# The 16-head transformer of a four-stage kernel: order of the down product, the scores, the residual sum and the keys' sum within a pair of slots

## The reference

```python
def local_attention(q, k, v):          # windows of w = 32, keys of this and the last window
    ...
    sim = jnp.einsum('bhwie,bhwje->bhwij', bq, bk2) * QK_SCALE
    sim = jnp.where(mask, -jnp.finfo(sim.dtype).max, sim)
    attn = jax.nn.softmax(sim, -1)
    out = jnp.einsum('bhwij,bhwje->bhwie', attn, bv2)
    ...
def attn_layer(x, Wqkv, qs, ksc, Wo):
    ...
    q = l2norm(q) * qs
    k = l2norm(k) * ksc
    ...
    q = q * cos * scale + rotate_half(q) * sin * scale
    k = k * cos * inv + rotate_half(k) * sin * inv
    out = local_attention(q, k, v)
    ...
    return out @ Wo
def ffn_layer(x, g, bln, W1, b1, W2, b2):
    mu = x.mean(-1, keepdims=True)
    var = ((x - mu) ** 2).mean(-1, keepdims=True)
    xn = (x - mu) / jnp.sqrt(var + 1e-05) * g + bln
    hg = xn @ W1 + b1
    a, gate = jnp.split(hg, 2, -1)
    return a * jax.nn.gelu(gate, approximate=False) @ W2 + b2
for i in range(DEPTH):
    x = attn_layer(shift_tokens(x), Wqkv[i], q_scale[i], k_scale[i], Wo[i]) + x
    x = ffn_layer(shift_tokens(x), ln_g[i], ln_b[i], W1[i], b1[i], W2[i], b2[i]) + x
```

## Time and profile before

| what | value |
|---|---|
| median of 3 runs | 3959.9 us (3956.89 to 3961.77) |
| the profiled execution | 3960.3 us, its span 3958.6 us |
| mean granted clock of TensorE | 0.963 |
| PE, DVE, ACT, POOL busy over the span | 89%, 63%, 58%, 45% |
| the touched stage | 1489.3 to 3319.3 us of the span (first and last maximum of the scores) |
| a pair of slots in it | about 19.0 us |

### The profile page before, as it was taken

How to read it: one execution, slowest core, us unless ns; L and a number is a source line. 1 busy time by engine, 2 the same in 40 slices (tenths; PEclk the granted TensorE clock), 3 DMA queues, 4 the chain that set the end, 5 groups by cost and what they waited for, 6 DMA issues and landing times. The chain is left out here.

```text
span 3958.6 us, 124976 instructions
## 1 busy us (share of the span) xinstructions
PE 3533.2 (89%) x52653; PEld 2411.9 (61%) x52653; DVE 2475.5 (63%) x5535; ACT 2290.3 (58%) x4664; POOL 1779.9 (45%) x1846
## 2 busy tenths in 40 slices
PE   7986999998999978999999999999999996968886
PEld 4664555544666645666666666666666665846664
DVE  4436554511666646776777777777677774568885
ACT  2233555522455546676666676666667665447775
POOL 2003000001011226666666666666666663167773
PEclk9997999998899989999999999999999998989998
DMA  0000000010000012112112112211211111121010
GB/s 26 2 3 24 1 1 1 1 30 7 2 2 2 2 35 74 46 45 71 45 47 69 46 47 56 61 47 45 71 46 46 45 46 27 30 78 24 21 23 20
DMA packets 156330, 130.09 MB, mean 33 GB/s; under 512 B 53592, under 2 KB 146304, under 8 KB 154880
## 3 DMA queue, kind: packets, MB, share of 16 engines
q1 hardware_dynamic: 155776, 122.09, 12.0%
HBM read 31.93 MB, written 3.54 MB: 9 GB/s over the span
## 5 line engine op out<-in xcount | busy, mean ns | idle before, releaser
L1072 PE MATMUL t_wa<-t_w_qkv,t_resid 128*128 128x512 f32 x1152 | 596.0, 617 | 22.3 <-DMA t_scales<-in_L_ffn_k_scale 18.9
L1387 DVE TENSOR_REDUCE t_nmax<-t_S 128x8 f32<-128x512 f32 x192 | 132.8, 692 | 358.6 <-PE t_S L1094 358.0
L1221 ACT ACTIVATE t_sq<-t_wa 128x512 f32<-128x512 f32 x384 | 216.3, 589 | 162.3 <-PE t_wa L1072 162.3
L1027 POOL TENSOR_TENSOR t_ra<-t_ra,t_rb 128x512 f32<-128x512 f32 x192 | 243.8, 1270 | 119.8 <-DVE t_rb L1345 119.8
L1327 DVE TENSOR_REDUCE t_ssq<-t_sq 128x8 f32<-128x512 f32 x384 | 261.0, 680 | 46.1 <-ACT t_sq L1221 46.1
L3079 DVE TENSOR_REDUCE a_nmax<-a_A 128x2 f32<-128x1024 f32 (+3 forms) x256 | 206.1, 822 | 127.0 <-PE a_A L2977 124.7
L1140 PE MATMUL t_misc<-t_oT,t_w_o 128*128 128x128 f32 x1536 | 194.2, 280 | 97.2 <-DVE t_resid L1376 97.2
L1256 ACT ACTIVATE t_oT<-t_T 128x512 f32<-128x512 f32 x192 | 114.8, 598 | 280.4 <-PE t_T L1129 280.3
L1020 POOL TENSOR_TENSOR t_rstd<-t_vare,half 128x1 f32<-128x1 f32 x96 | 52.9, 551 | 481.1 <-DVE t_vare L1398 481.1
L1110 PEld LDWEIGHTS t_T<-ident,t_ra 128*128 128x128 f32 x1536 | 177.3, 141 | 139.4 <-issue 105.0
L1072 PEld LDWEIGHTS t_wa<-t_w_qkv,t_resid 128*128 128x128 f32 x1152 | 188.1, 196 | 119.4 <-issue 95.3
(11 more groups left out here) (506 smaller groups left out, 9841.5 us busy)
## 6 DMA issues: line engine op xcount, KB each, us to landing
t_vw<-t_vn SPq DMA_DIRECT2D x768, 66.0 KB
t_vw<-t_vn SPq DMA_DIRECT2D x672, 33.0 KB
t_w_qkv<-in_L_ffn_Wqkv SPq DMA_DIRECT2D x6, 1536.0 KB, 6.6
t_v<-t_vn SPq DMA_DIRECT2D x56, 132.0 KB, 2.3
t_vw<-t_nothing SPq DMA_DIRECT2D x96, 33.0 KB
t_w_o<-in_L_ffn_Wo SPq DMA_DIRECT2D x6, 512.0 KB
f_h<-t_L_ffn_h_w SPq DMA_DIRECT2D x2, 1024.0 KB, 7.3
t_w<-in_L_ffn_W SPq DMA_DIRECT2D x6, 341.0 KB
```

The costliest lines, as they stand in the source:

```text
L1027: pool.tensor_tensor(ra[:, ahead % 2, 0], ra[:, ahead % 2, 0], rb[:, ahead % 2, 0], ALU.add).then_inc(q_added.sem, 1)
L1072: pe.matmul(bank, resid[:, b, lo:lo + P], w_qkv[:, l % 2, at:at + 512], start=True, stop=True).then_inc(wa_up.sem, 1)
L1221: act.activation(sq[:, r].rearrange("p h d -> p (h d)"), wa[:, WA[kind], :], ACT.Square).then_inc(squared.sem, 1)
```

## The change

No operation is added or taken away; the order of steps changes on three engines.

PE: in an even slot down comes ahead of turn_p instead of behind it. gate_up is cut into half_up(gate) and half_up(up), and the scores of the next (even) slot stand between the two, at the end of the odd slot, instead of at the head of the even one.

ACT, even slots: copy_q moves between the two squares, and copy_k ahead of the roots.

DVE, even slots: add_ffn moves from behind floor to behind the queries' sum, ahead of rotate_queries; the keys' sum and floor move behind the outputs; normalise_keys moves into the following odd slot, behind add_heads. In odd slots make_tables moves from the head of the slot to behind normalise_keys.

```diff
--- before.py
+++ after.py
@@ -1149,14 +1149,13 @@
                     pe.wait_ge(lnd.sem, lnd.at(t, 4))
                     pe.transpose(lnP, ln[:, :], ident[:, :]).then_inc(lnT_up.sem, 1)
 
-                def gate_up(t):
-                    l = layer_of(t)
+                def half_up(t, kind):
+                    l, half = layer_of(t), int(kind == "gate")
                     pe.wait_ge(lnT_in.sem, lnT_in.at(t, 1))
-                    for half, kind in ((1, "gate"), (0, "up")):
-                        bank = turn_bank(kind, t)
-                        for c in range(NH):
-                            m = pe.matmul(bank[:, c * P:(c + 1) * P], w_1[:, l % 2, half, c * P:(c + 1) * P], lnT[:, :], start=True, stop=True)
-                        m.then_inc(T_up.sem, 1)
+                    bank = turn_bank(kind, t)
+                    for c in range(NH):
+                        m = pe.matmul(bank[:, c * P:(c + 1) * P], w_1[:, l % 2, half, c * P:(c + 1) * P], lnT[:, :], start=True, stop=True)
+                    m.then_inc(T_up.sem, 1)
 
                 def down(t):
                     l = layer_of(t)
@@ -1166,7 +1165,7 @@
                     m.then_inc(f_up.sem, 1)
 
                 for even, now, turn, mid, ahead, tail, ffn, last in slots():
-                    if now is not None:
+                    if now is not None and (not even or last is None):
                         score(now)
                     if ahead is not None:
                         project("q", ahead)
@@ -1177,10 +1176,10 @@
                     if turn is not None:
                         turn_qk("q", turn)
                     if even:
+                        if last is not None:
+                            down(last)
                         if now is not None:
                             turn_p(now)
-                        if last is not None:
-                            down(last)
                         if turn is not None:
                             turn_qk("k", turn)
                         if now is not None:
@@ -1205,7 +1204,10 @@
                         if now is not None:
                             turn_o(now)
                         if ffn is not None:
-                            gate_up(ffn)
+                            half_up(ffn, "gate")
+                            if now is not None and now + 1 < TG:
+                                score(now + 1)
+                            half_up(ffn, "up")
 
             @block.scalar
             def _(act):
@@ -1274,13 +1276,18 @@
                             exponentials(now)
                         if ahead is not None:
                             square("q", ahead)
-                            square("k", ahead)
                         if turn is not None:
                             copy_q(turn)
+                        if ahead is not None:
+                            square("k", ahead)
                         if now is not None:
                             copy_p(now)
                         if mid is not None:
                             copy_v(mid)
+                        if turn is not None:
+                            copy_k(turn)
+                        if ahead is not None:
+                            roots(ahead)
                     else:
                         if ahead is not None:
                             square("q", ahead)
@@ -1294,10 +1301,10 @@
                             copy_q(turn)
                         if mid is not None:
                             copy_v(mid)
-                    if ahead is not None:
-                        roots(ahead)
-                    if turn is not None:
-                        copy_k(turn)
+                        if ahead is not None:
+                            roots(ahead)
+                        if turn is not None:
+                            copy_k(turn)
                     if ffn is not None:
                         norm_turned(ffn)
                     if now is not None:
@@ -1376,45 +1383,68 @@
                         v.scalar_tensor_tensor(out=resid[rows, b, cols], in0=fT[rows], scalar=b_2[rows, l % 2, :],
                                                in1=resid1[rows, b, cols], op0=ALU.add, op1=ALU.add).then_inc(tile_done.sem, 1)
 
+                def weights(G):
+                    scores = S[:, :, 0:4 * KEYS].rearrange("p r (h k) -> p r h k", h=4)
+                    v.wait_ge(scored.sem, scored.at(G))
+                    v.tensor_reduce(nmax[:, :, :], scores, X, ALU.max).then_inc(maxed.sem, 1)
+                    v.wait_ge(maxed.sem, maxed.at(G))
+                    v.tensor_tensor(p.rearrange("p j r k -> p r j k"), scores, spread(nmax[:, :, :], 3, KEYS), ALU.subtract).then_inc(subbed.sem, 1)
+
+                def outputs(G):
+                    out = S[:, :, 0:4 * VD].rearrange("p r (h d) -> p r h d", h=4)
+                    v.wait_ge(weighed.sem, weighed.at(G))
+                    v.reciprocal(rden[:, :, :], out[:, :, :, HD]).then_inc(recip.sem, 1)
+                    v.wait_ge(recip.sem, recip.at(G))
+                    v.tensor_tensor(o.rearrange("p j r d -> p r j d"), out[:, :, :, 0:HD], spread(rden[:, :, :], 3, HD), ALU.mult).then_inc(o_in.sem, 1)
+
+                def statistics(t):
+                    v.wait_ge(sh2_up.sem, sh2_up.at(t))
+                    v.bn_stats(stats[:, :], sh2).then_inc(lnd.sem, 1)
+                    v.wait_ge(lnd.sem, lnd.at(t, 1))
+                    v.bn_aggr(mv[:, :], stats[:, :]).then_inc(lnd.sem, 1)
+                    v.wait_ge(lnd.sem, lnd.at(t, 2))
+                    v.tensor_scalar(vare[:, :], mv[:, 1:2], LN_EPS, None, ALU.add).then_inc(lnd.sem, 1)
+
                 for even, now, turn, mid, ahead, tail, ffn, last in slots():
-                    if ahead is not None and ahead % SLOTS == 0:
-                        make_tables(layer_of(tile_of(ahead)))
-                    if ffn is not None:
-                        add_heads(ffn)
-                    if now is not None:
-                        scores = S[:, :, 0:4 * KEYS].rearrange("p r (h k) -> p r h k", h=4)
-                        v.wait_ge(scored.sem, scored.at(now))
-                        v.tensor_reduce(nmax[:, :, :], scores, X, ALU.max).then_inc(maxed.sem, 1)
-                        v.wait_ge(maxed.sem, maxed.at(now))
-                        v.tensor_tensor(p.rearrange("p j r k -> p r j k"), scores, spread(nmax[:, :, :], 3, KEYS), ALU.subtract).then_inc(subbed.sem, 1)
-                    if last is not None:
-                        gated(last)
-                    if ffn is not None:
-                        v.wait_ge(sh2_up.sem, sh2_up.at(ffn))
-                        v.bn_stats(stats[:, :], sh2).then_inc(lnd.sem, 1)
-                        v.wait_ge(lnd.sem, lnd.at(ffn, 1))
-                        v.bn_aggr(mv[:, :], stats[:, :]).then_inc(lnd.sem, 1)
-                        v.wait_ge(lnd.sem, lnd.at(ffn, 2))
-                        v.tensor_scalar(vare[:, :], mv[:, 1:2], LN_EPS, None, ALU.add).then_inc(lnd.sem, 1)
-                    if ahead is not None:
-                        sums("q", ahead)
-                    if ahead is not None:
-                        rotate_queries(ahead)
-                        sums("k", ahead)
-                        floor(ahead)
-                    if last is not None:
-                        add_ffn(last)
-                    if ffn is not None:
-                        v.wait_ge(rooted.sem, rooted.at(ffn))
-                        v.tensor_scalar(ln[:, :], sh2, mv[:, 0:1], rstd[:, 0:1], ALU.subtract, ALU.mult).then_inc(lnd.sem, 1)
-                    if now is not None:
-                        out = S[:, :, 0:4 * VD].rearrange("p r (h d) -> p r h d", h=4)
-                        v.wait_ge(weighed.sem, weighed.at(now))
-                        v.reciprocal(rden[:, :, :], out[:, :, :, HD]).then_inc(recip.sem, 1)
-                        v.wait_ge(recip.sem, recip.at(now))
-                        v.tensor_tensor(o.rearrange("p j r d -> p r j d"), out[:, :, :, 0:HD], spread(rden[:, :, :], 3, HD), ALU.mult).then_inc(o_in.sem, 1)
-                    if ahead is not None:
-                        normalise_keys(ahead)
+                    if even:
+                        if now is not None:
+                            weights(now)
+                        if last is not None:
+                            gated(last)
+                        if ahead is not None:
+                            sums("q", ahead)
+                        if last is not None:
+                            add_ffn(last)
+                        if ahead is not None:
+                            rotate_queries(ahead)
+                        if now is not None:
+                            outputs(now)
+                        if ahead is not None:
+                            sums("k", ahead)
+                            floor(ahead)
+                    else:
+                        if ffn is not None:
```

(21 more changed lines are left out.)

## The result

The changed kernel takes 3853.3 us, the median of four runs at 3846.5, 3847.9, 3858.6 and 4089.6 us, of which the last ran at a granted clock of 0.83 and is left out of the comparison. The kernel before took 3958.4 in the runs beside it. The ratio of the changed kernel's time to that of the one before is 0.973, its 95% interval 0.9705 to 0.9755: 107 us less, where 95 were forecast. The profiled execution took 3847.9 us.

What follows compares the result with a forecast made beforehand. PE was taken to bound the stage, idle mainly ahead of L1140 for DVE's late residual. 94 pairs by 1.07 us, less 6 for the tables, gave 94.6 off 3960.3: 3865 us, bounds 3855 to 3878, range 3850 to 3895.

Steps and rivals of the forecast that it cites:

- the replay: One pair's steps retimed on its own clock from profile durations: pair goes from 19.05 to 17.98 us.
- The sum's main term: PE's wait ahead of head product L1140 goes: 1.07 us in each of 94 pairs, 100.6 us.
- The 0.21: Weigh's start behind copy_p's end in the kernel before, read as ACT's copy fixing that start.
- The tables: make_tables behind normalise_keys on DVE costs about 1.2 us in each of five pairs, 6 us.
- the lower bound of my sum: 96 pairs winning 1.10 us each and no cost of the tables: 3855 us.
- the margin that I left below: The range was the forecast's 3855 to 3878, extended down to 3850.
- weigh is bound by ACT and not won upon: ACT's copy_p fixes weigh's start, again at 2206.75; nothing is won ahead of it, PE rests some 0.4 us there.
- the early scores only hold the margin of down: Early scores make down's input ready by 2203.70, so turn_p ends 0.10 us before ACT is free for it.
- DVE becomes the bound behind weigh: Rival: DVE's chain from queries' sum to odd maximum runs late; 0.5 us a pair gives 3912; chance 0.13.
- the 0.15 that I gave it: DVE's replayed rest between normalise_keys' end (2210.90) and the odd maximum's due time (2211.05), in us.
- slower: Rival: normalise_keys ends late and holds the odd slot's softmax; 1.5 us late loses 23 us, 3984; chance 0.04.
- The rival that the wait moves: PE would wait as long elsewhere, for the turned outputs or turn_p: 3960, no change; chance 0.05.

Runs made afterwards that it cites:

- experiment 8: Changed kernel with the keys' sum and floor back ahead of the outputs on DVE in even slots: 3867.3 us, ratio 0.9759 to the kernel before.
- experiment 9: Changed kernel with make_tables of a new layer moved behind gated in the even slot, in DVE's rest: 3853.6 us, ratio 0.9714 to the kernel before.
- experiment 12: Changed kernel with copy_p ahead of the keys' square, plus w_qkv's load in six transfers, one a slot, other weights eight slots later: 3811.4 us.
- experiment 10: Changed kernel with copy_p ahead of the keys' square on ACT in even slots: 3822.7 us, ratio 0.9646 to the kernel before.
- experiments 6 and 7: Changed kernel with scores back at the head and gate and up in one piece: 3867.8 us; the same with down also back behind turn_p: 3861.1 us.
- experiment 4: Changed kernel with down back behind turn_p on PE: 3845.9 us, ratio 0.972 to the kernel before.
- experiment 5: Changed kernel with down back behind turn_p and copy_p ahead of the keys' square: 3843.6 us, against 3822.7 with down ahead.
- experiment 1: Kernel before with one move alone, add_ffn behind the queries' sum on DVE: 3916.3 us, ratio 0.9894.
- experiment 2: Kernel before with PE's moves alone (down ahead of turn_p, scores between gate and up): 3982.4 us, ratio 1.0065.
- experiment 3: Kernel before with the scores between gate and up alone, down staying behind turn_p: 3939.4 us, ratio 0.9944.
- experiment 11: Changed kernel with ACT's even slot as square q, exponentials, copy_q, copy_p, square k: 3850.9 us, ratio 0.9711 to the kernel before.

## Why the prediction was right

The change does what the replay said, and in the order in which it said it.

The sum's main term, 1.07 us a pair, measured 1.15 (17.83 us a pair, where 17.98 was said of one of 19.05): weigh started 0.15 behind copy_p's end instead of 0.21, and the step behind it after 0.78 instead of 0.80. I had taken the middle between 1.04 and 1.10; the truth is just above both. The 0.21 was a misreading. In the kernel before it wasn't ACT that fixed the start of weigh at 2206.75, but PE's own order: weigh stood, without rest, behind the turned keys, 0.07 us later than copy_p would have let it, and the turned keys had waited for copy_q:

```profile
2206.19 0.63 PE L1110 MATMUL t_T<-ident,t_ra 128*128 128x128 f32 x4 [0.19 <-ACT t_qT L1248]
```

Down ahead of turn_p and copy_q one operation earlier brought the turned keys forward (5.24 instead of 5.73), and only then was copy_p the bound. That ACT would hold weigh after the change was right; that it did before was not.

The tables were taken with 1.2 us in five pairs; they measured 1.54 (19.37 us against 17.83). POOL and DVE where the second layer begins, in the changed kernel:

```profile
1748.71 1.04 POOL L1030 TENSOR_TENSOR t_ra<-t_ra,t_inv 128x512 f32<-128x512 f32 x1 [0.95 <-ACT t_inv L1237]
...
1749.40 0.64 DVE L1326 TENSOR_TENSOR t_rot<-t_base,t_scales 128x256 f32<-128x256 f32 x1
...
1750.36 0.41 DVE L1326 TENSOR_TENSOR t_rot<-t_base,t_scales 128x256 f32<-128x256 f32 x1
...
1751.10 0.68 DVE L1389 TENSOR_REDUCE t_nmax<-t_S 128x8 f32<-128x512 f32 x1
```

The multiplications hold the odd maximum back until 1751.10, which is 12.03 us behind the pair's table load instead of 10.50. Of the 0.3 us by which the tables cost more than forecast, 0.2 are a meeting with POOL: its L1030 runs until 1749.75, and the first multiplication takes 0.64 us instead of 0.42. The other 0.1 is that the odd maximum, without tables, was due at 10.50 and not at 10.58 as replayed (2211.05, with the pair's table load at 2200.47), so there was less rest to hide in. In experiment 8, where L1030 ended ahead of the first multiplication, this takes 0.42 us; in experiment 9 the meeting is seen by itself. The Trainium skill (SBUF — State Buffer, section "SBUF: two separate sides") says that a VectorE operation with two SBUF inputs and a GpSimd operation that reads SBUF lock one another out; the trace agrees, and by that rule the sum would have had these 0.2 us a pair more.

Not in the sum at all were the pairs with a load: 14.2 us longer together (with the pair behind each) instead of 20.6, which is 6 us of the gain. They moved between 0.4 and 25 us from one order to the next, which no term of mine held; experiment 12 shows that they are a matter of their own. With 91 x 1.15 = 104.6, less 7.3 for the tables, plus 6.4 for the loads, the stage's 105.2 us are accounted for to within 2. The time itself, 3853.3, is 12 us under the forecast and 2 under the lower bound of my sum; it lies in the range by the margin that I left below. The profiled execution was forecast at 3865.7 and took 3847.9, 18 us less. Some 6 of them are the loads' and 6 lie outside the stage; both are luck, since no term of the sum foresaw them. The others are the main term's.

That weigh is bound by ACT and not won upon was right (33.8 us of rest there, and experiment 10). That the early scores only hold the margin of down was right in kind, but the margin was larger than said: the turned probabilities end at 5.08, 0.4 ahead of copy_p and not 0.10, for the turned queries start at 3.36 instead of 3.61 now that PE no longer waits ahead of up. By experiments 6 and 7 PE's moves are worth 8 to 15 us all the same, and by experiment 4 not the place of down but that of the scores.

The rival "DVE becomes the bound behind weigh" was nearer than its time says: the odd maximum has under 0.1 us of rest, and experiment 5 shows each 0.3 us on that chain costing 0.3 us a pair. It was not reached: the operations on DVE had the lengths of the rows, and the maximum kept 0.08 us of the 0.15 that I gave it. The rival "slower" by normalise_keys didn't happen: the inverse norms end at 9.50, while add_heads, which stands ahead of normalise_keys, ends at 9.69. The rival that the wait moves is the case of experiment 1, in part.

## What to carry to other kernels

Ask of a wait not only which instruction ends it but what that instruction had ahead of it on its own engine: here the residual's product was ready 1.8 us before its turn, and moving it past the operations that nobody waited for, and the keys' sum out of the way of the outputs, gave 2.7%. The residual's move alone brought 0.50 of the 1.15 us a pair, and all moves but that of the keys' sum 0.90. Replay the engine's order on the clock of one pair with the durations of the trace, one rest after another, and count every rest on the way, for an edit that costs nothing may only be hidden by the bound next to it. After it look at what PE waits for now: the copy that it names was worth another 30 us for one exchanged line.

## What the runs showed of the hardware

TensorE's granted clock fell to its lower level inside a steady loop, in 24 of 95 pairs, when PE rested up to 0.69 us in one piece and 1.04 us shortly behind (experiment 2): 1.6 us a time, and a kernel 26 us slower than before. With six matmuls within the first rest (experiment 3) it did not fall in these pairs. DVE's multiplication of two SBUF inputs took up to 1.49 us instead of 0.41 beside POOL's additions. And a burst of weights (1536 KB and some more in one slot) stopped PE amid a run of matmuls, for 3.4 us in the changed kernel and up to 5.0 in experiment 11; it went on 1.2 to 1.6 us after a 16 KB packet of the instruction queue had landed, and behind the stop of 3.4 us the clock fell.
